# Layer 1's own attention and the first own attention of layer 2's block: a batch's last product in the next batch's first gap, the next values' projection ahead of the divisors

## What is computed

```
def _mha(x, y, ...):
    xn = _ln(x, lnx_g, lnx_b); yn = _ln(y, lny_g, lny_b)
    q, k, v = xn @ wq, yn @ wk, yn @ wv            # 16 heads of 32
    a = softmax(q k^T * 32 ** -0.5)
    if causal: a = a * mask                        # masked after the softmax
    x_out = x + (a v) @ li1_w + li1_b
    h = gelu(_ln(x_out, ln3_g, ln3_b) @ li2_w + li2_b)
    return x_out + h @ li3_w + li3_b
x = _ln(xx, ln1_g, ln1_b)
x = x + _mha(x, x, ..., causal=True)
```

## Time and profile before

| | |
|---|---|
| median of 3 runs | 2333.48 us (2329.95 to 2341.6) |
| the profiled execution | 2332.43 us, span 2331.1 us, granted clock 0.86 |
| PE busy | 2032.0 us, 87% |
| DVE busy | 1355.2 us, 58% |
| ACT busy | 895.1 us, 38% |
| POOL busy | 554.5 us, 24% |
| DMA | mean 25 GB/s |
| chain that ended last | PE 70%, DVE 11%, issue 9%, ACT 5%, POOL 4% |

### The profile page before, as it was taken

One profiled execution on the slowest core, in us unless ns is written; L12 is line 12 of the kernel. 1 busy time (PEld: TensorE's weight loads), 2 busy tenths in 40 slices (PEclk: granted clock), 3 DMA queues, 4 the chain that ended last, 5 costly groups with the idle time before them and its releaser, 6 DMA issues.

```text
span 2331.1 us, 57677 instructions
## 1 busy us (share of the span) xinstructions
PE 2032.0 (87%) x22720; PEld 1478.6 (63%) x22720; DVE 1355.2 (58%) x3605; ACT 895.1 (38%) x3421; POOL 554.5 (24%) x1355
## 2 busy tenths in 40 slices
PE   8999998989977998998967887998999997789744
PEld 4899998867565665566856654665654544556522
DVE  6666676755255787445636614876262300678797
ACT  2455554533155564302334522665111111256511
POOL 3566664222011000102425502331000000401111
PEclk9555555999988998999988998999999999889965
DMA  3000001004000002000030000000030000000000
GB/s 135 4 5 5 5 5 78 1 5 177 0 2 8 12 12 103 34 1 23 1 129 1 2 1 11 8 11 2 9 141 1 0 0 1 1 18 12 2 0 16
DMA packets 8027, 57.22 MB, mean 25 GB/s; under 512 B 792, under 2 KB 5248, under 8 KB 5984
## 3 DMA queue, kind: packets, MB, share of 16 engines
q1 hardware_dynamic: 7760, 53.54, 6.0%
HBM read 52.62 MB, written 0.92 MB: 23 GB/s over the span
## 4 chain that ended last, share of the span: by engine, by line
PE 70%; DVE 11%; issue 9%; ACT 5%; POOL 4%; DMA 1%; POOLq 0%; DVEq 0%; SPq 0%; ACTq 0%
PE banks L259 43%; PE banks L1339 9%; PE banks L264 8%; PE banks L912 3%; ACT memory L960 2%; PE banks L938 2%; PE banks L1492 1%; DVE memory L1222 1%; DVE memory L799 1%; DVE memory L1441 1%; POOL memory L3194 1%; PE banks L1643 1%; PE banks L1620 1%; ACT memory L1366 1%; POOL memory L1398 1%
## 5 line engine op out<-in xcount | busy, mean ns | idle before, releaser
L259 PE MATMUL banks<-memory 128*112 128x256 f32 (+7 forms) x4192 | 1139.7, 428 | 71.2 <-POOL memory L2048 8.0
L259 PEld LDWEIGHTS banks<-memory 128*128 128x128 f32 (+3 forms) x4192 | 710.4, 197 | 404.1 <-issue 259.8
L264 PE MATMUL banks<-memory 112*125 112x112 f32 (+3 forms) x2000 | 303.4, 284 | 117.4 <-DVE memory L799 66.6
L264 PEld LDWEIGHTS banks<-memory 112*125 112x125 f32 (+3 forms) x2000 | 236.7, 171 | 234.0 <-issue 136.2
L1339 PE MATMUL banks<-memory 128*128 128x8 bf16 (+2 forms) x10752 | 312.5, 175 | 8.8 <-DVE memory L1424 1.4
L1339 PEld LDWEIGHTS banks<-memory 128*128 128x128 bf16 x10752 | 299.9, 104 | 22.0 <-POOL memory L1398 13.0
L960 ACT ACTIVATE memory<-banks,memory 112x375 f32<-112x375 f32 x384 | 215.1, 577 | 19.9 <-DVE memory L998 19.8
L998 DVE TENSOR_REDUCE memory<-banks 112x2 f32<-112x750 f32 x192 | 171.1, 934 | 38.8 <-PE banks L912 38.6
L1441 DVE TENSOR_REDUCE memory<-banks 128x48 f32<-128x192 f32 x448 | 122.0, 291 | 62.2 <-PE banks L1339 43.1
L815 POOL TENSOR_TENSOR memory<-memory 112x1 f32<-112x1 f32 x72 | 39.6, 550 | 416.5 <-DVE memory L794 415.1
L1006 DVE COPY memory<-banks 125x448 f32<-125x448 f32 x192 | 117.1, 620 | 10.2 <-PE banks L264 5.9
(11 more groups left out here) (234 smaller groups left out, 2415.9 us busy)
## 6 DMA issues: line engine op xcount, KB each, us to landing
memory<-in_l2x SPq DMA_DIRECT2D x1, 7680.0 KB, 21.6
memory<-in_l2f SPq DMA_DIRECT2D x1, 7168.0 KB, 19.7
memory<-in_l1f SPq DMA_DIRECT2D x1, 4617.0 KB, 15.6
memory<-in_ctxT SPq DMA_DIRECT2D x24, 187.5 KB
memory<-in_l2f SPq DMA_DIRECT2D x1, 4096.0 KB, 12.7
memory<-in_l3f SPq DMA_DIRECT2D x1, 3073.0 KB, 22.0
memory<-in_l2a SPq DMA_DIRECT2D x1, 3072.0 KB, 19.2
memory<-in_l0f SPq DMA_DIRECT2D x1, 2304.0 KB, 9.0
```

Source lines behind the costliest of these rows:

```text
L259: ins = self.nc.tensor.matmul(out, weights[i], acts[i], start=i == 0, stop=i == n - 1)
L264: return self.nc.tensor.transpose(out, in_, self.ident[0:n, 0:n])
```

## The change

Only the lists of steps of `L1Attn` and of `L2Block1` are written anew; no instruction is added, taken out or changed in size. In both `y` of batch b moves from gap 4 of its own batch to gap 0 of the next, and in the last batch to `tail`. In both `v` of the next batch moves from gap 2, ahead of `share` and `all`, to gap 3, behind `weights` and ahead of `inverse`. In `L1Attn` `stats` moves from gap 2 to 0, `xn` from 3 to 2, `xT` from 4 to 3. In `L2Block1` `stats3` moves from gap 4 to gap 1 of the next batch, there behind `xm`; `xn3` from gap 0 to 2, ahead of `stats`; `xT3` from gap 2 to 3.

```diff
--- before.py
+++ after.py
@@ -1993,9 +1993,9 @@
     scale, k_pieces, key_step, share, near, qm = 0.25, 1, 2, 0.6, True, None
     prologue = (("stats", 0), ("xn", 0), ("xT", 0), ("parity", 0), ("k", 0), ("q", 0))
     second = (("v", 0, 0), ("stats", 0, 1), ("xn", 0, 1), ("xT", 0, 1))
-    plan = ((("k", 0, 1),), (("q", 0, 1), ("near", 0, 0)), (("v", 0, 1), ("stats", 0, 2)), (("xn", 0, 2),),
-            (("xT", 0, 2), ("y", 0, 0)))
-    tail = ()
+    plan = ((("y", 0, -1), ("k", 0, 1), ("stats", 0, 2)), (("q", 0, 1), ("near", 0, 0)), (("xn", 0, 2),),
+            (("v", 0, 1), ("xT", 0, 2)), ())
+    tail = (("y", 0),)
 
     def __init__(self, k):
         super().__init__(k)
@@ -2304,9 +2304,9 @@
     lib, ln, ln3 = 4, 0, 8
     prologue = (("ln", 0), ("xm", 0), ("stats", 0), ("xn", 0), ("xT", 0), ("k", 0), ("q", 0))
     second = (("v", 0, 0), ("ln", 0, 1), ("xm", 0, 1), ("stats", 0, 1), ("xn", 0, 1), ("xT", 0, 1))
-    plan = ((("k", 0, 1), ("xn3", 0, -1), ("ln", 0, 2)), (("q", 0, 1), ("xm", 0, 2)),
-            (("v", 0, 1), ("xT3", 0, -1), ("stats", 0, 2)), (("xn", 0, 2),), (("xT", 0, 2), ("y", 0, 0), ("stats3", 0, 0)))
-    tail = (("xn3", 0), ("xT3", 0))
+    plan = ((("y", 0, -1), ("k", 0, 1), ("ln", 0, 2)), (("q", 0, 1), ("xm", 0, 2), ("stats3", 0, -1)),
+            (("xn3", 0, -1), ("stats", 0, 2)), (("v", 0, 1), ("xT3", 0, -1), ("xn", 0, 2)), (("xT", 0, 2),))
+    tail = (("y", 0), ("stats3", 0), ("xn3", 0), ("xT3", 0))
 
     def __init__(self, k):
         self.keep = k.upper
```

## The result

The changed kernel takes 2356.07 us (median of 4 runs, 2355.1 to 2357.81) against 2332.9 for the kernel before (4 runs): a ratio of 1.0095, with a 95% interval of 1.008 to 1.0111. It is slower by 23 us; 2369 was forecast, with a range of 2348 to 2384.

A forecast was written before the change was run, and what follows sets the result against it. PE, busiest at 87%, was taken as the bound except at three stalls per batch. Layer 1 -4, block's waits +30.5, clock +10 made +36.5 us: 2369 us, own range 2353 to 2381, 8-in-10 range 2348 to 2384.

The forecast's parts named there:

- The two stages' signs: Layer 1's own attention faster by 4 us; layer 2's block slower by 30.5 us at full clock plus 10 of clock.
- the waits: Layer 1: PE stalls of 1.18 us before `inverse` and 0.92 before `y`, 2.10 a batch against 2.53.
- I leave their number: Layer 1: count of slow-clock stretches taken as unchanged, bounded by none (-8 us) and one per batch (+3).
- ACT's queue (A): Block: ACT copies `v` behind 16 exponentials, 6.61 us after the maxima begin, and `inverse` waits for it.
- POOL's and DVE's queue (B): Block: `stats3`'s pow queues behind `xm`'s three POOL operations; maxima start some 5.3 us after q ends instead of 3.9.
- The sum of waits: Block at full clock: batch 0 +3.0 us, five batches +5.3 each, batch 6 +1; together +30.5 us.
- The clock's term in the block: Block: `inverse`, `products` and `y` at 1.2 GHz, 2.4 us in each of seven batches, less today's 6.8: +10 us.
- Only ACT's order counts: Rival, 13%: block's `xn3` isn't late, maxima start when `all` ends; +1.7 us a batch, 2350 us.
- The clock stays low longer: Rival, 15%: block's `k` and turns are slow in each batch too, 12 us more, 2381 us.
- The plan pays: Rival, 3%: block's `v` copy is ready with the divisors, PE loses three stalls; with layer 1 some 2309 us.
- The clock behind the long wait: Block: clock halves after an idle stretch, so each of seven batches has a slow stretch behind its long wait.

The follow-up runs named there:

- `stats3` ahead of `ln`: Changed kernel, but in the block `stats3` and `xn3` stand in gap 0 ahead of `ln`, and `xm` ahead of q: 2349.14 us.
- `y` moved: Layer 1 as changed; block's old lists, but `y` in the next batch's gap 0 with `stats3`, `xn3` behind it, ahead of `ln`: 2317.1 us.

## Why the prediction was right, and where its sizes were off

Forecast +36.5 us, measured +23 by the medians and +25.4 by the profiled spans; within the range, and on the forecast side.

- **The two stages' signs: right.** -4 was forecast for layer 1 and +40.5 for the block; -7.2 and +34.7 came.
- **Layer 1: the waits right, the clock not.** Stalls of 2.10 us a batch were forecast, 1.24 + 0.79 = 2.03 came; a full-clock batch is 10.96 us against 10.95 forecast (11.55 less 0.6), which for six batches is the forecast's 3.5 us. "I leave their number" was the step that failed, of the slow stretches: they fell from five to three, which is 2.8 us of the 7.2. The first batch and the end, taken to break even, brought 0.9 more (-1.5 and +0.6). PE's busy time over a stretch of each stage, windows of before and of after:

```profile
651.00:763.00 112.00, 84.92 (x900) 68.48 (x900) 62.00 (x173) 63.24 (x303) 15.15 (x26) 0.87 0.02 5
1214.00:1359.00 145.00, 107.68 (x1023) 82.25 (x1016) 82.01 (x233) 64.27 (x296) 68.98 (x91) 0.87 0.02 8
```

```profile
652.00:757.00 105.00, 80.02 (x904) 65.80 (x901) 62.46 (x173) 62.78 (x303) 15.49 (x26) 0.91 0.02 5
1208.00:1387.00 179.00, 112.53 (x1018) 87.70 (x1011) 78.79 (x233) 63.53 (x295) 68.98 (x91) 0.81 0.02 6
```

  In layer 1 it falls by 4.9 us, but that isn't all gain: the opening's projection of `v` takes 1.12 us instead of 2.01, and PE waits for DVE's `xn` right behind it in both.
- **ACT's queue (A): right.** Forecast: maxima to copied `v` 6.61 us, measured 1281.75 - 1275.19 = 6.56; idle 7.4, measured 7.06. (The prediction has today's copy end "about when the maxima begin"; it ends 1.2 us ahead of them, at 1285.40. No term rests on that.) The row of the stage's opening carried this over to every batch unchanged. Two kernels that differ from the changed one in A alone (`v` copied by DVE, `v` back in gap 2) give back 29 and 32 us of stage, and one that moves only `v` loses all of it.
- **POOL's and DVE's queue (B): right.** Maxima at q's end + 5.16, forecast 5.29. Its worth with A present is 9.7 us of stage (the changed kernel against `stats3` ahead of `ln`), or 2.0 us of PE's waiting in a batch. Without A no pair of kernels isolates it: `v` back in gap 2 and `y` moved (146.7 and 139.6 us) differ also in the place of `xT3`, whose copy costs 1.08 us there.
- **The sum of waits: right.** +30.5 forecast; the stage's +34.7 less PE's longer busy time, 112.53 - 107.68 = 4.9, leaves 29.8. By windows, each less PE's longer busy time, batch 0 lost 3.4 us (forecast 3.0), batches 1 to 4 4.9 each and batch 5 4.3 (forecast 5.3), and the opening and the end 2.6 together (forecast 1).
- **The clock's term in the block: too large.** +10 forecast, +4.9 measured. The 2.4 us per batch were right where they were meant (five windows of after have a mean PE busy time of 14.4 us, 2.5 above the 11.99 of the earlier trace rows), but I counted seven batches: in the sixth window PE's busy time is 11.97 us against 11.53, so it has hardly any excess, and the end of the stage was as slow before. Of the 11 us between forecast and spans, 6 are the block's (5 of them this term), 3 layer 1's and 2 the untouched stages'; all three lie on the same side, so no errors cancel in it. The bounds given for the block's clock and for layer 1 add up to 2351 to 2385, not quite to the 2353 to 2381 stated.
- **The rivals.** "Only ACT's order counts" gave 2350, nearer to the measured 2356 than the forecast itself. That is luck: it put the block's waits at 12 us where 29.8 came, and part of the missing 18 was hidden by a clock's term that was 5 too large and a gain in layer 1 that was 3 too small. The trace and the `stats3` run show both queues at work. "The clock stays low longer" asked for 12 us more on the clock's term; PE's busy time grew by 4.9 in all. "The plan pays" was right of the idea and wrong of the place: with `v` where ACT can copy it ahead of the exponentials, and `y` moved, the kernel takes 2310 to 2317 us.
- **The clock behind the long wait.** Behind the idle 7.06 us `inverse` and `products` take 0.98 and 1.72 us at a granted clock of 0.50. With the rule that the prediction cites from the Trainium skill, "TensorE: Matmul & The Clock Gate", section "Part 1: The HAM clock gate", the trace agrees: every batch with the long wait has its slow stretch behind it.

## What to carry to other kernels

A step that is moved within one list of steps is moved in every engine's queue: before moving a projection, ask which engine copies its result and what that engine has in front of the copy then. Where banks are handed out in turn, the copy releases a step two places on, so a late copy stops work that doesn't use its result. Look for a place in the old trace, an opening or an end, that already has the new order: here one row there gave the time from the maxima to the copied `v` within 1%.

## What the runs showed of the hardware

- PE's clock can fall behind small waits. In the kernel before, `y` takes 3.4 to 3.5 us in four of six batches and 1.95 in another, in three of the four behind the same waits as in the fast one (1.28, 1.26 or 1.27, and 0.35 us). With one more POOL operation the first of them grew to 1.51 us, the granted clock fell from 0.90 or 1.00 to 0.79 to 0.81 in all six batches, and these became 0.6 to 2.4 us longer; 9 us in the stage, seen in the median too (+8). In layer 1, with 0.5 us of stalls less per batch, two of five slow stretches went away, 2.8 us. PE's order of work changed there as well, so the part of the stalls isn't separated.
- Behind an idle stretch of 7.06 us PE's busy time of a batch was 13.7 to 15.0 us in four batches, where 11.99 is that at full clock.
- DVE's norm L799 takes 0.41 us by itself and 1.20 beside POOL's mask, for the same shape; the mask takes 1.10 instead of 0.98 where it starts second.
